# Two aggregations of an adjacency-graph chain: three 16 bit parts against two parts in the rounded 32 bit type

## The reference

```python
x = _layernorm(x + _L0_gnn_ref(x, adj, ...))   # softmax attention; the adjacency is an additive mask
x = _layernorm(x + _L1_gnn_ref(x, adj, W, b))  # (adj / neighbours) @ x, then @ W.T + b, leaky relu
x = _layernorm(x + _L2_gnn_ref(x, adj, W, a))  # 4-head graph attention, softmax over the neighbours
x = _layernorm(x + _L3_gnn_ref(x, adj, B))     # D^-1/2 (adj + I) D^-1/2 @ x, then @ B
```

## Time and profile before

| what | value |
|---|---|
| median of 3 runs | 984.38 us (983.39 to 985.41) |
| the profiled execution, its span | 984.94 us, 983.1 us |
| PE busy | 875.9 us, 89% of the span |
| DVE busy | 778.0 us, 79% |
| ACT busy | 468.3 us, 48% |
| POOL busy | 329.0 us, 33% |

### The profile page before, as it was taken

How to read it: one execution, slowest core, us unless ns; L and a number is a source line. 1 busy time by engine, 2 the same in 40 slices (tenths; PEclk the granted TensorE clock), 3 DMA queues, 4 the chain that set the end, 5 groups by cost and what they waited for, 6 DMA issues and landing times.

```text
span 983.1 us, 25627 instructions
## 1 busy us (share of the span) xinstructions
PE 875.9 (89%) x11097; PEld 656.8 (67%) x11112; DVE 778.0 (79%) x1699; ACT 468.3 (48%) x540; POOL 329.0 (33%) x335
## 2 busy tenths in 40 slices
PE   4997999998998989989999989989899898993875
PEld 2654689555975669656895569756696568951872
DVE  4438788788987889868887889878898688886975
ACT  1542682446615665246734466156652567316500
POOL 2021430624133521616206251334216162054512
PEclk9998999999999999999999999999999999997887
DMA  9741210651127120441205411171204412000200
GB/s 183 122 90 19 65 45 4 108 108 44 46 36 128 55 65 25 87 91 40 88 3 104 112 44 46 31 135 52 65 25 88 88 43 65 4 1 23 66 3 22
DMA packets 98880, 60.63 MB, mean 62 GB/s; under 512 B 69040, under 2 KB 86576, under 8 KB 98768
## 3 DMA queue, kind: packets, MB, share of 16 engines
q1 hardware_dynamic: 89280, 41.69, 17.9%
q0 software_dynamic: 8448, 16.78, 9.6%
q10 hardware_dynamic: 1040, 0.52, 0.2%
HBM read 54.66 MB, written 4.33 MB: 60 GB/s over the span
## 4 chain that ended last, share of the span: by engine, by line
PE 66%; DVE 20%; issue 4%; ACT 4%; DMA 3%; POOL 1%; POOLq 0%; DVEq 0%; ACTq 0%
PE ring L1208 19%; PE Z L1224 12%; PE Z L1176 8%; PE ring L1154 8%; PE ring L1189 8%; DVE x L795 6%; DVE cmat L759 4%; DMA adj<-in_adj_dram 3%; PE ring L1238 2%; PE ring L1152 2%; DVE ring L704 2%; PE ring L1092 2%; PE ring L1119 1%; ACT steps L611 1%; DVE meanvar L788 1%
## 5 line engine op out<-in xcount | busy, mean ns | idle before, releaser
L611 ACT ACTIVATE steps<-sjrow,steepsi 128x1024 bf16<-128x1024 f32 x248 | 268.2, 1139 | 123.1 <-DVE cmat L759 85.1
L759 DVE TENSOR_TENSOR cmat<-steps,adj 128x1024 f16<-128x1024 bf16 x180 | 153.7, 897 | 24.5 <-ACT steps L611 22.6
L1208 PE MATMUL ring<-vparts,cmat 128*128 128x66 bf16 x4416 | 146.4, 195 | 18.4 <-DVE cmat L759 12.1
L1176 PEld LDWEIGHTS Z<-vv,probs 128*128 128x128 f32 x1024 | 122.6, 191 | 52.6 <-ACT probs L618 37.3
L1208 PEld LDWEIGHTS ring<-vparts,cmat 128*128 128x128 f16 x4416 | 143.9, 99 | 19.7 <-issue 7.2
L440 POOL TENSOR_SCALAR vareps<-meanvar 128x4 f32<-128x4 f32 x64 | 13.4, 210 | 415.2 <-DVE meanvar L788 414.3
L1176 PE MATMUL Z<-vv,probs 128*128 128x129 f32 x1024 | 126.5, 277 | 25.4 <-ACT probs L618 25.4
L1154 PE MATMUL ring<-qT,xT 128*128 128x512 f32 x256 | 139.7, 628 | 0.0
L618 ACT ACTIVATE probs<-ring 128x1024 f32<-128x1024 f32 x64 | 65.2, 1018 | 65.9 <-PE ring L1154 65.9
L704 DVE CUSTOM_DVE_ANT_0 ring<-ring,maskb 128x1024 f32<-128x1024 f32 x64 | 78.5, 1229 | 22.7 <-PE ring L1092 22.6
L1224 PE MATMUL Z<-adjT,vparts 128*128 128x512 f16 x384 | 88.8, 386 | 7.9 <-DVE vparts L809 7.9
(11 more groups left out here) (126 smaller groups left out, 1262.5 us busy)
## 6 DMA issues: line engine op xcount, KB each, us to landing
adj<-in_adj_dram POOLq DMA_DIRECT2D x16, 1024.0 KB, 12.6
sjrow<-sj_rows SPq DMA_DIRECT2D x31, 512.0 KB, 4.0
out_dram<-x SPq DMA_DIRECT2D x16, 256.0 KB, 2.4
x<-in_x_dram SPq DMA_DIRECT2D x7, 512.0 KB, 4.4
adjT<-adj SPq DMA_TRANSPOSE x64, 3.4
x<-in_x_dram ACTq DMA_DIRECT2D x1, 512.0 KB, 4.3
sjbuf<-in_a_dram SPq DMA_DIRECT2D x1, 128.0 KB, 10.6
sj_rows<-sjbuf SPq DMA_DIRECT2D x8, 16.0 KB
```

The costliest lines, as they stand in the source:

```text
L611: act.activation(steps[:, n % STEPS, :], sjrow[:, h % 2, :], ACT.Relu, bias=steepsi[:, t, h:h + 1], scale=STEEP).then_inc(step_made, 1)
L759: dve.tensor_tensor(c_of[:, t, :], steps[:, n % STEPS, :], adjs[o.parity][:, t, :], ALU.min)\
L1176: last = pe.matmul(zq[:, q, 0:D + 1], probs[:, n % 2, j, q * P:(q + 1) * P], vv[:, kt, :], start=kt == 0 and q % 2 == 0, stop=kt == T - 1, ...
L1208: last = pe.matmul(s[:, jt, 0:VW], c_of[:, t, jt * P:(jt + 1) * P], vparts[:, t, h, part, :], start=t == 0 and part == 0, stop=t == T - 1 ...
```

## The change

Both aggregations take their operands in the rounded 32 bit type (`float32r`), which keeps fewer digits than 32 bit, so that two parts hold a value where three of bf16 were needed. Both operands have to be of that type, so the transposed adjacency is widened tile by tile by ACT, into one buffer of 8 tiles, `wide_low` (tiles 0 to 3, its own space) and `wide_high` (tiles 4 to 7, in the space of `cmat[:, 0]`). To make space there is only one `adjT`: it serves agg1, and for agg3 the older graph's adjacency is transposed a second time, into `cmat[:, 1]`, once head 1 has been used. The parts and three small buffers share space with others.

```diff
-        adjTs = [sb(f"adjT{p}", [P, T, N], F16) for p in range(2)]
+        adjT = sb("adjT", [P, T, N], F16)
+        wide_low = sb("wide_low", [P, T // 2, N], F32R)
...
+        wide_high = sharing("wide_high", [P, T // 2, N], F32R)
         cmat = sb("cmat", [P, 2, T, N], F16)
+        adjT_of_older = cmat[:, 1, :, :]
...
             def turn_adj(g):
-                if g.base >= 2:
-                    sp.wait_ge(read["agg3"], g.before(2).count(2, 2))
+                if g.base > 0:
+                    sp.wait_ge(widened["agg1"], g.count(T))
...
+            def turn_older(o):
+                sp.wait_ge(full["c"], o.count(2 * H, 4))
+                for t in range(T):
+                    sp.dma_start_transpose(adjT_of_older[:, :, t * P:(t + 1) * P], adjs[o.parity][:, t, :])\
+                        .then_inc(turned_older, 16)
...
             def add_diagonal(g):
-                pool.wait_ge(full["agg1"], g.count(2, 2))
-                blocks = diagonal_blocks(adjTs[g.parity])
+                pool.wait_ge(turned_older, g.count(16 * T, 16 * T))
+                blocks = diagonal_blocks(adjT_of_older)
...
+            def widen(kind, g, agg, tiles):
+                for t in tiles:
+                    if agg == "agg1" and t == 0:
+                        act.wait_ge(turned, g.count(16 * T, 16 * T))
+                    if agg == "agg3" and t == 0:
+                        act.wait_ge(diag_added, g.count(1, 1))
+                    if t < T - 1 and (agg == "agg3" or g.base > 0):
+                        act.wait_ge(wide_used, uses_until(agg, g, t))
+                    if t == T // 2 and kind == "full" and agg == "agg1":
+                        act.wait_ge(full["c"], g.before().count(2 * H, 2 * H))
...
+                    act.activation(wide(t), src, ACT.Copy).then_inc(widened[agg], 1)
...
                 dve.tensor_copy(parts[:, 0, ts, :], src).then_inc(done, 1)
                 dve.wait_ge(done, g.count(per, at + 1))
-                dve.tensor_tensor(left, src, parts[:, 0, ts, :], ALU.subtract).then_inc(done, 1)
-                dve.wait_ge(done, g.count(per, at + 2))
-                dve.tensor_copy(parts[:, 1, ts, :], left).then_inc(done, 1)
-                dve.wait_ge(done, g.count(per, at + 3))
-                dve.tensor_tensor(parts[:, 2, ts, :], left, parts[:, 1, ts, :], ALU.subtract).then_inc(done, 1)
+                dve.tensor_tensor(parts[:, 1, ts, :], src, parts[:, 0, ts, :].bitcast(F32), ALU.subtract).then_inc(done, 1)
...
+                early = [(c, t) for c in range(2) for t in range(T // 2)]
+                late = [(c, t) for c in range(2) for t in range(T // 2, T)]
+                if agg == "agg1":
+                    early = [(c, t) for t in range(T // 2) for c in range(2)]
+                for c, t in early + late:
+                    if c == 0:
+                        pe.wait_ge(widened[agg], of.count(T, t + 1))
...
-                    for part in range(3):
-                        last = pe.matmul(Z[:, c, :], parts[:, part, t, :], mat[:, t, c * 512:(c + 1) * 512],
+                    for part in range(2):
+                        last = pe.matmul(Z[:, c, :], parts[:, part, t, :], wide(t)[:, c * 512:(c + 1) * 512],
```

More of the change, by code:

```diff
@@ L37 @@
 F32 = mybir.dt.float32
+F32R = mybir.dt.float32r
 F16 = mybir.dt.float16
@@ L224, in gnn_kernel @@
         x_in = sem("x_in")
-        turned = [sem(f"adj_turned{p}") for p in range(2)]
+        turned = sem("adj_turned")
+        turned_older = sem("adj_turned_older")
+        widened = {n: sem(f"{n}_widened") for n in ("agg1", "agg3")}
+        wide_used = sem("wide_used")
         adj_in = [[sem(f"adj_in{p}_half{k}") for k in range(2)] for p in range(2)]
@@ L388, in step @@
                     sp.dma_start(x0[:, :, :], x_v[number(Graph(g.base + 1))]).then_inc(x_in, 16)
+                if kind != "first":
+                    turn_older(o)
             program(step)
@@ L569, in take_sums @@
                     act.activation(dst[:, c * 512:(c + 1) * 512], Z[:, c, :], ACT.Copy).then_inc(read[name], 1)
+            def widen(kind, g, agg, tiles):
[8 more added lines that the diff above has]
+                        act.wait_ge(full["c"], g.before().count(2 * H, 2 * H))
+                    if t == T // 2 and kind == "last":
+                        act.wait_ge(full["c"], g.count(2 * H, 2))
+                    src = adjT[:, t, :] if agg == "agg1" else adjT_of_older[:, t, :]
+                    act.activation(wide(t), src, ACT.Copy).then_inc(widened[agg], 1)
             def take_group(kind, g, name, k):
@@ L623, in step @@
                     take_group(kind, g, name, k)
+                if kind == "full" and g.base > 1:
+                    make_maskb(g, range(4, T))
                 made = 0
@@ L640, in step @@
                             made += PACE[n]
-                    if kind == "first":
-                        make_maskb(Graph(1), range(4, T))
-                if kind != "first":
-                    for n in range(made, len(STEP_TILES[kind])):
-                        step_tile(kind, o, n)
-                if kind != "last":
-                    take_sums("agg1", g, agg1T)
-                for c in range(2):
-                    if kind == "full" and (g.base < NB - 1):
-                        make_maskb(Graph(g.base + 1), range(4 * c, 4 * c + 4))
-                    if kind != "first":
-                        take_sums("agg3", o, agg3T, [c])
+                if kind == "first":
+                    widen(kind, g, "agg1", range(T))
+                    take_sums("agg1", g, agg1T)
+                    make_maskb(Graph(1), range(4, T))
+                    return
+                for n in range(made, len(STEP_TILES[kind])):
+                    step_tile(kind, o, n)
+                if kind == "full":
+                    widen(kind, g, "agg1", range(T))
+                    take_sums("agg1", g, agg1T, [0])
+                    widen(kind, o, "agg3", [0])
+                    take_sums("agg1", g, agg1T, [1])
+                    widen(kind, o, "agg3", range(1, T))
+                else:
+                    widen(kind, o, "agg3", range(T))
+                take_sums("agg3", o, agg3T)
+                if kind == "full" and g.base < NB - 1:
+                    make_maskb(Graph(g.base + 1), range(0, 4))
             program(step)
@@ L819, in split_x3 @@
                 if k == 1:
-                    dve.wait_ge(split3, o.count(10, 5))
+                    dve.wait_ge(split3, o.count(6, 3))
                 for j in range(4):
@@ L1241, in layer1 @@
             def layer1(kind, g):
-                pe.wait_ge(split1, g.count(8, 4))
+                pe.wait_ge(split1, g.count(4, 2))
                 pe.wait_ge(y_made[0], g.count(2, 2))
-                pe.wait_ge(turned[g.parity], g.count_own(16 * T, 16 * T))
-                aggregate(kind, g, g, "agg1", "out1", parts1, adjTs[g.parity], (split1, g.count(8, 8)), agg1T, w1_s)
+                aggregate(kind, g, g, "agg1", "out1", parts1, (split1, g.count(4, 4)), agg1T, w1_s)
             def finish_layer1(kind, g):
```

60 lines of the change are left out of this document (32 added, 28 removed).

## The result

| | median, us | runs |
|---|---|---|
| kernel before, same chip | 985.41 | 983.39 to 985.79 (5) |
| changed kernel | 978.63 | 977.33 to 981.10 (5) |

The ratio is 0.9948, with a 95% interval of 0.9930 to 0.9965: faster, but by under 1%; that is some 5 us by the ratio (3.4 to 6.9 by its interval) and 6.8 by the medians, where 11.8 were forecast. The profiled execution of the changed kernel, the fastest of its five, took 977.33 us, with a span of 975.5; that of before 983.1, so the two traces differ by 7.6 us, and these are what has to be accounted for. ACT is now busy for 587.1 us (60%), PE for 848.5 (87%).

The account below looks back on a forecast made before the run. PE's products were taken to hold most of the chain, with ACT having room. Gains of 10.5, 2.5, 2.9 and 3.3 made 19.2 us, less 7.4 for the clock: 11.8, so a median of 972.6 us, range 957 to 987.

Parts of the forecast that it names:

- SP and POOL: Second transposes land at 1.0 us after agg1's start, then POOL's diagonal, scales and degrees; DVE's chain stays covered.
- The product's price: PE's aggregations: a rounded-type product takes 0.23 us (ends 0.216 and 0.45), so each aggregation saves 3.0 us.
- (4): Rival: rounded-type products stream columns at the 32 bit pass's pace, 0.45 us; about +80, 1065 us, slower; chance 0.12.
- (5): Rival: the 32 bit weight load, 193 ns, is not hidden; a product costs 0.41 us, about 1044 in all; chance 0.05.
- Agg3 at ACT's pace: In agg3 PE follows ACT's widening; second out3 starts at 20.05 us, 4.3 earlier, of some 6 that PE saved.
- the mask ahead of xT: Four mask tiles on ACT before its xT copy: q starts 5.2 us after second out3, not 3.2, at 25.25.
- The opening's loss: The other four mask tiles, between sj and first probs, delay DVE's fifth guard row maximum: 1.07 us lost per opening.
- The clock's term: PE's 3.2 us idle ahead of q drops the clock at three of six openings, 2.47 us each: 7.4 us lost.
- The first step: In the first step agg1 saves 3.0 us and the mask tiles behind it take some back: 2.5 us gained.
- rival (3): Second transposes land 2 us later; POOL's chain sets the first guard score, some 1.7 us at seven places: 984.5; chance 0.08.
- 0.3 to spare: Full step: DVE's chain behind POOL's degrees ends at 28.1 us, q's cast cannot begin before 28.4, so it is covered.
- the terms 2.9 and 3.3: Gains of 2.9 us at the boundary of graph 7 to the last step and 3.3 us in the last step.

## Why the prediction was right, and where not

The step that failed is that of SP and POOL, the last point below.

- **The product's price** held: 0.234 us for 0.23. Rivals (4) and (5), the 32 bit pace and a weight load that shows, are out. A load of 197 ns lay beside products 234 ns apart with every product on all rows of the array; the sentence of the Trainium skill (TensorE: Matmul & The Clock Gate, Part 3, The mechanism) that a load overlaps with products in flight "only when row_grp differs" does not hold for this row, nor for the earlier trace rows. The same section also lets a load into the background weight buffer go ahead, and with that the rows agree; the forecast, which made (5) follow from the one sentence, left this out.
- **Agg3 at ACT's pace, and the mask ahead of xT,** gave marks within 0.2 us (19.99 and 25.05). The reason given for the first was too strong: without ACT's widening it would have been 18.93. The opening's loss held: from s0 to the second scores of layer 0 it is 12.63 in the opening of graph 2, where it was 11.56: 1.07, as forecast.
- **The clock's term** came out in sum by luck, and was wrong in both factors. I had 2.47 us at three of six openings, 7.4; in the changed kernel's six steps s0 stands at 30.28 to 30.73, on the mean 30.52, which is 1.27 above the 29.25 of an undisturbed step: 7.6. The clock fell at all six (q took 2.45 to 3.56 us, not 1.96). But in four of them, graphs 3 to 6, DVE's cast of q did not wait for ACT: it stands right behind the cast of x, at the end of the chain that POOL's late degrees hold. In graph 3's opening (t = 0 at 278.61) ACT was done with qT at 307.26, 1.2 us before the cast began:

```profile
306.14 1.12 ACT L624 ACTIVATE qT<-ring,bqcol 128x1024 f32<-128x1024 f32 x1 [2.63 <-PE ring L1122]
...
307.82 0.68 DVE L1007 CAST qxb<-xT 128x1024 bf16<-128x1024 f32 x1
308.43 0.68 DVE L1011 CAST qxb<-qT 128x1024 bf16<-128x1024 f32 x1
```

  So two causes lie over each other, and without any fall of the clock DVE's chain alone would have cost some 6.4 of the 7.6. This is an estimate: by when the cast of x let go of DVE, the cast of q could have begun 0.8, 1.6, 0.8, 1.7, 1.4 and 0 us behind the 28.19 of an undisturbed step. The 2.47 came from 192 products in a head; behind q only q, v and the cast wait, and they lose less. How many of six openings are hit I can't derive: an idle time of 3.05 us (2.50 to 3.06 in the changed kernel) was followed by a fall at six, five, four, three, two and one of them in six kernels.
- **The first step** gave 4.36 for 2.5. Before, PE stood idle for 4.79 us ahead of s0, and the guard scores behind it ran at the low clock; from s0 to the first scores took 9.52. Now the idle time lies ahead of q, the low clock falls on q and v, and that distance is 8.22.
- **SP and POOL is the step that failed.** It took the price of the first transposes, 10.90 to issue and 3.4 to land, for the second ones, which run in another place: 11.63 to 13.78, and 4.5. So the diagonal came at 1.5 to 5.2, not at 1.0. This was rival (3), where the "0.3 to spare" was gone; it had priced it at 1.7 us in each of seven steps. In the full steps it came too, at four openings of six, but together with the fall of the clock, which the sum had already counted, so little more was lost. At the boundary and in the last step no mask tiles stand in the way, nothing covers POOL's chain, and the terms 2.9 and 3.3 went to -0.10 in sum. Putting the scales first gave 6.12 back there, and earlier transposes 11.74. Two of the forecast's own signs of being wrong came with it: drstd 6.4 us in at graph 4's step and 8.7 at graph 7's, and s0 1.5 to 1.9 us earlier, not 2 to 3. The direction stood, and so did the product's price, ACT's part and the mask's; two terms out of five were mis-sized, by 6.3 us, of which the first step made up 1.9.

## What to carry to other kernels

A duration belongs to the place that it was measured in: before a DMA's price is moved to another stretch, look at what else uses the DMA engines there, instruction fetches among them. A step that waits for a transfer goes behind the work in its queue that doesn't need the transfer; here one line moved was worth more than the change itself. And a slack of 0.3 us in a sum of twenty terms is no cover: the places where nothing else hides the chain (here the boundary and the last step) are where its error is paid in full. Last, a sum that comes out right in one stretch doesn't show its terms: here the clock and POOL's chain held the same mark, and only the experiments told them apart.

## What the runs showed of the hardware

- Fetches of instructions hold up DMA transposes. Where blocks of instructions were fetched in the heads, the transposes' rate went from about 200 GB/s to 10 or less, four times in one stretch, for up to 1.3 us. The fetches took 1.9% of the engines' time in that stretch and the engines were all but idle in the stops (0 to 2 tenths), so it isn't the engines' time that was short; what held the transposes no run shows.
- DVE's scaling of half of x3 (L869) takes 1.10 us; with the scales first, that of the second half runs beside POOL's addition of the diagonal and took 2.91 at the boundary:

```profile
852.34 2.91 DVE L869 TENSOR_SCALAR rest<-x,meanvar,drstd 128x128 f32<-128x128 f32 x4
```

  In the changed kernel's order the addition is over by then, and the same scaling took 1.12 at the boundary. The Trainium skill (GPSIMD Engine Reference, 1. Specifications) says that GpSimd shares its interfaces to SBUF with VectorE, with contention for DVE instructions in a 2-port mode or with two inputs in SBUF. These rows agree that the two contend; whether L869 is one of these forms no run shows.
- Eleven products that compute nothing, in each of seven steps, made the kernel 4.9 us faster by the medians (966.09 to 961.18), by keeping the clock up over a wait. Without them the runs lay from 960.83 to 967.38, with them from 959.50 to 961.68.
